# A four-layer decoder on one core: GpSimd's convolution taps placed behind each group's variance root in the first attention block

## The chip, the cores and the metric

The kernel runs on one core of a Trainium2 chip. The metric is the device time of the whole program in microseconds (us), as the median of runs. The engines are called as in the profile: PE (TensorE) multiplies matrices, DVE (VectorE) and ACT (ScalarE) work element by element and can read the results of PE, POOL (GpSimd) works on memory only, and SP (SyncE) issues transfers. Each engine runs its own instructions in order, and waits on semaphores for the others. All transfers of this stage are issued by SP.

## The reference

A decoder of four layers over 16 sequences of 128 tokens with 128 channels. Every layer has three blocks (attention, cross attention, feed-forward), and every block ends in `x = layernorm(x + block(x))`. The first attention block is

```
qkv = x @ W_qkv                                  # 16 heads of 8 channels
attn = softmax(mask(q @ k.T * SCALE))            # inside chunks of 64 tokens, causal
out_local = attn @ v
cross = sigmoid(q . mean_k(previous chunks) * SCALE)
out = (out_local + cross * cum_mean_v * 0.5) @ W_out
x = layernorm(x + out)                           # (x - mean) / sqrt(var + 1e-5)
```

The last layer's cross attention holds a long convolution (a diagonal state-space filter) whose 128 taps a channel depend on weights alone:

```
dtA = exp(log_dt) * (A_re + i A_im);  dC = C * (exp(dtA) - 1) / A
taps[d, l] = 2 * Re(sum_n dC[d, n] * exp(dtA[d, n] * l)),  n = 64 states, l = 0..127
```

with the skip weight added to the first tap.

## The kernel before, in words

`program` (L5379) runs the blocks one behind the other. Each is a `stage` (L35): five instruction streams between two common barriers. The change is in `small_heads` (L763), which makes the first attention (`local` is true) and the second layer's cross attention (`local` is false).

The 16 sequences go in four groups g = 0 to 3 of four sequences. A group has 16 units (head sets), and a written-out order of slots t sets what each engine does: at slot t PE makes the scores of one unit and the turned scores of a unit six slots older, DVE takes the maxima (`peak`, L1082), ACT the exponentials (`exp`, L1004), and one "misc" item of a group is made: input turned (`x`), projections (`q`, `k`, `v`), maxima and sums turned (`mt`, `ot`, L921), the output projection with the residual (`fin`, L981). The misc items share three PSUM banks in rotation, so an item waits until the item three before it has been moved out. DVE's `key_means` (L1090) makes the chunk means of the keys.

The layer norm of a group is spread over three engines:
- DVE's `moments(g)` takes statistics from the `fin` bank and aggregates them to mean and variance (`mv`, L1141), one slot behind `fin`.
- POOL computes the root of the variance: `rs = (var + eps) ** -0.5` and `nb = -mean * rs`, four small instructions (L1191 to L1197), here called root g. They wait for the variances of group g, and for g > 0 until the `fin` bank of group g − 1 was moved.
- ACT's `apply(g)` (L1051), three slots behind `fin`, writes `x_all` from the bank with that scale and bias. ACT's next exponential stands behind it, and the bank is free only then.

Besides, POOL computes in this stage the taps of the last layer's convolution, in class `Taps` (L610): `angles` and `powers` (L683 to L746) make tables of powers of the states, `low` (16 powers) and `high` (8). `taps(pool, a)` (L748) makes 16 of the 128 taps, for a = 0 to 7: one product over 128 x 2048 elements (L655), six halving sums (L658), one last sum to `kern`, and for a = 0 the skip. After a = 7 a small memset raises `made`, on which SP stores `kern` to DRAM (`store`, L635 to L638). Each instruction of the chain waits for the one before it.

POOL's order in this stage is: masks, `angles`, `powers`, taps 0 and 1, root 0, taps 2 and 3, root 1, taps 4 and 5, root 2, taps 6 and 7, root 3. SP's is: the parameters of the taps, the next block's weights, the store of the taps.

Of the kernel before, what the change touches and what calls it, by code (L numbers as in the profile page):

```python
# [762 lines left out]
def small_heads(K, pre, local):  # L763
# [10 lines left out]
    with ExitStack() as es:  # L774
# [64 lines left out]
        with stage(nc, *names) as (block, loaded, const_step, inited, pool_step, masks, filled, moved0, moved1, moved2, a_done, maxed, b_done, exped, o_done,  # L839
# [6 lines left out]
            s4d = Taps(K, sb, taps_loaded, dt_ready, angle, curves_made, tap_step, taps_made, taps_stored) if local else None  # L846

            @block.sync
            def _(sp):
                if local:  # L850
                    s4d.fetch(sp)
                    with nc.allow_non_contiguous_dma(reason="small parameter columns"):
                        K.w_l0_xattn.fetch(sp, I, next_in)
                    s4d.store(sp)
                    sp.wait_ge(next_in, 16 * K.w_l0_xattn.N)
                else:
                    for dst, n in ((wq_, "Wq"), (wk_, "Wk"), (wv_, "Wv"), (wo, "Wo")):
                        sp.dma_start(dst[:], I[pre + n]).then_inc(loaded, 16)
                    sp.dma_start(bo[:], row(I[pre + "bo"])).then_inc(loaded, 16)
# [303 lines left out]
            @block.gpsimd  # L1163
            def _(pool):
                if local:
                    build = Chain(pool, pool_step)
                    for full, low, turned in ((half_mask, mask16, False), (half_mask_t, mask_t16, True)):
                        sign = -1 if not turned else 1
                        build(nc.gpsimd.memset(full[:], 0.0))
                        for z in range(2):  # L1170
                            part = full[CS * z:CS * z + CS, :]
                            build(nc.gpsimd.affine_select(out=part, in_=part, compare_op=ALU.is_ge, fill=NEG, base=0,
                                                          pattern=[[sign, CS]], channel_multiplier=-sign))
                        build(nc.gpsimd.tensor_copy(low[:], full[:]))
                    build(nc.gpsimd.memset(to_next[:], 0.0))
                    nc.gpsimd.memset(to_next[0:CS, CS:T], 0.25 / CS).then_inc(masks, 1)
                    nc.gpsimd.memset(pT[:], 0.0).then_inc(masks, 1)
                    s4d.begin(pool)
                    s4d.angles(pool)
                    s4d.powers(pool)  # L1180
                for g in range(NG):
                    if local and g:
                        s4d.taps(pool, 2 * g)
                        s4d.taps(pool, 2 * g + 1)
                    if local and g == 0:
                        s4d.taps(pool, 0)
                        s4d.taps(pool, 1)
                    pool.wait_ge(var_ready, G * (g + 1))
                    if g:
                        wait_moved(pool, "fin", g - 1)  # L1190
                    nc.gpsimd.tensor_scalar(rs[:], mv[:, :, 1], EPS, None, ALU.add).then_inc(rstd_step, 1)  # L1191
                    pool.wait_ge(rstd_step, 3 * g + 1)
                    nc.gpsimd.tensor_tensor(rs[:], rs[:], K.minus_half[:, 0:G], ALU.pow).then_inc(rstd_step, 1)
                    pool.wait_ge(rstd_step, 3 * g + 2)
                    nc.gpsimd.tensor_scalar(nb[:], mv[:, :, 0], -1.0, 1.0, ALU.mult, ALU.mult).then_inc(rstd_step, 1)
                    pool.wait_ge(rstd_step, 3 * g + 3)
                    nc.gpsimd.tensor_tensor(nb[:], nb[:], rs[:], ALU.mult).then_inc(rstd_ready, 1)  # L1197
# [4248 lines left out]
```

## Time and profile before

| | us |
|---|---|
| median of 3 runs | 5502.06 (5499.12 to 5502.11) |
| profiled execution, its time | 5501.84 |
| its span, first to last instruction | 5500.1 |
| PE busy | 4484.7 (82%) |
| DVE busy | 3591.8 (65%) |
| ACT busy | 2738.8 (50%) |
| POOL busy | 2465.6 (45%) |
| mean granted clock of PE | 0.897 of full |

The busy times are of all twelve blocks together. The first attention block takes the stretch from 6 to 218 us of the span; ACT's first instruction of the next one starts at 220.25. A timeline row gives the start, the duration, the engine, the line, the operation, the tile written and the tiles read, the shapes, how many equal instructions were merged, and in brackets the idle time before it with what ended it. Where instructions of one line are merged, the duration is that of all of them. A row by stretches gives the stretch, its length, then the busy us and (in brackets) the instructions of PE, of PE's weight loads, of DVE, ACT and POOL, then the granted clock as a share of full (0.50 is 1.2 GHz, 1.00 is 2.4 GHz), and the share and GB/s of the DMA engines. In a list of waits, "A <- B" means that A's instruction waited for B's. In the code that follows a program's tile `s4prod` appears in rows as `l_attn_s4prod`.

### The profile page before, as it was taken

How to read it: one execution, taken by the hardware profiler on the slowest of the kernel's cores; microseconds unless marked ns; L12 is line 12 of the kernel's file. 1: busy time of each engine (PE TensorE's matmuls, PEld its weight loads, DVE VectorE, ACT ScalarE, POOL GpSimd, SP SyncE). 2: the span in 40 equal slices, each digit the busy share in tenths (PEclk: the TensorE clock that was granted, in tenths of full speed). 3: DMA queues.
4: the chain of work that ended last, by engine and by line, in shares of the span. 5: the costliest groups of instructions: out<-in, count | busy, mean ns of one | idle time of the engine just before them, and what ended most of it. 6: DMA issues, size and time to landing. Idle time of an engine off the chain costs nothing. (4 is left out here: it accounts for less than half of the span.)

```text
span 5500.1 us, 116174 instructions
## 1 busy us (share of the span) xinstructions
PE 4484.7 (82%) x45623; PEld 2775.8 (50%) x45624; DVE 3591.8 (65%) x6873; ACT 2738.8 (50%) x4638; POOL 2465.6 (45%) x2282
## 2 busy tenths in 40 slices
PE   7768999999999999678647888877887689967577
PEld 5545666666666666336523334343563444424344
DVE  4347777777777776475286999999553436547355
ACT  3325666666666666553225656655553235533121
POOL 8436666666666665250275666666332210001100
PEclk7789999999999999788668999999998779977788
DMA  1001111111111111000000000000000000020000
GB/s 23 16 29 28 45 37 29 49 33 45 36 43 37 29 37 29 5 0 3 12 1 14 0 1 1 0 1 1 15 1 0 13 9 16 1 70 5 20 1 8
DMA packets 110396, 102.35 MB, mean 19 GB/s; under 512 B 37095, under 2 KB 80375, under 8 KB 109111
## 3 DMA queue, kind: packets, MB, share of 16 engines
q1 hardware_dynamic: 107831, 94.14, 6.9%
q8 instruction: 357, 5.85, 0.4%
q0 software_dynamic: 2048, 1.05, 0.1%
q14 instruction: 160, 1.31, 0.1%
HBM read 40.18 MB, written 1.18 MB: 8 GB/s over the span
## 5 line engine op out<-in xcount | busy, mean ns | idle before, releaser
L4201 POOL TENSOR_TENSOR l_attn_read<-l_attn_state,l_attn_c_rows 128x1024 f32<-128x1024 f32 x256 | 604.4, 2362 | 291.6 <-DVE l_attn_state L4103 174.4
L2999 POOL TENSOR_TENSOR l_ffn_t<-l_ffn_t 128x512 f32<-128x512 f32 x384 | 487.3, 1269 | 506.5 <-DVE l_ffn_t L2866 506.5
L2597 PE MATMUL psum<-l_ffn_wq,l_ffn_xsT 128*128 128x512 f32 x1152 | 599.6, 612 | 99.3 <-DVE l_ffn_t L2866 97.8
L3823 PE MATMUL psum<-l_attn_read,ident 128*128 128x512 f32 x1024 | 489.9, 596 | 7.3 <-DVE l_attn_yz L4111 5.0
L3005 POOL TENSOR_TENSOR l_ffn_t<-l_ffn_t,l_ffn_ss 128x512 f32<-128x512 f32 x384 | 400.5, 1043 | 0.7 <-DVE l_ffn_ss L2881 0.7
L2862 DVE TENSOR_TENSOR l_ffn_t<-psum,l_ffn_tab 128x512 f32<-128x512 f32 x384 | 258.8, 674 | 121.3 <-ACT l_ffn_sq L2748 118.6
L4103 DVE TENSOR_TENSOR_SCAN l_attn_state<-l_attn_decay,psum 128x1024 f32<-128x1024 f32 x144 | 329.0, 2285 | 4.5
L2645 PEld LDWEIGHTS psum<-l_ffn_pT,l_ffn_v 64*64 64x64 f32 x3072 | 248.8, 135 | 142.9 <-issue 138.8
L2597 PEld LDWEIGHTS psum<-l_ffn_wq,l_ffn_xsT 128*128 128x128 f32 x1152 | 179.4, 191 | 274.0 <-DVE l_ffn_t L2866 237.9
L3979 ACT ACTIVATE l_attn_decay<-l_attn_dt,l_attn_a 128x1016 f32<-128x1016 f32 x256 | 292.9, 1144 | 37.2 <-DVE l_attn_state L4100 33.8
L2645 PE MATMUL psum<-l_ffn_pT,l_ffn_v 64*64 64x64 f32 (+1 forms) x3072 | 306.1, 227 | 1.2 <-ACT l_ffn_pT L2764 1.2
L2645 PE MATMUL psum<-l_ffn_pT,l_ffn_vx 64*64 64x32 f32 (+1 forms) x6144 | 303.6, 217 | 0.0
L4004 ACT COPY l_attn_c_rows<-psum 128x512 f32<-128x512 f32 x256 | 149.4, 584 | 298.9 <-PE psum L3814 263.1
L2220 ACT ACTIVATE l_attn_pT<-psum 128x512 f32<-128x512 f32 x320 | 173.6, 594 | 240.8 <-PE psum L2118 170.8
L2645 PEld LDWEIGHTS psum<-l_ffn_pT,l_ffn_vx 64*64 64x64 f32 x6144 | 282.3, 135 | 0.0
L4100 DVE TENSOR_TENSOR_SCAN l_attn_state<-l_attn_decay,psum 128x512 f32<-128x512 f32 x224 | 261.6, 1208 | 31.2 <-PE psum L3853 26.8
L3814 PE MATMUL psum<-l_attn_parts,pick 96*128 96x512 bf16 x456 | 170.6, 390 | 136.3 <-DVE psum L4086 88.7
L2748 ACT ACTIVATE l_ffn_sq<-psum 128x512 f32<-128x512 f32 x384 | 229.6, 598 | 103.7 <-PE psum L2597 103.6
L3823 PEld LDWEIGHTS psum<-l_attn_read,ident 128*128 128x128 f32 x1024 | 195.5, 192 | 140.0 <-issue 116.8
L2771 ACT COPY l_ffn_oT<-psum 128x512 f32<-128x512 f32 x192 | 111.9, 583 | 305.9 <-PE psum L2645 305.8
L4086 DVE TENSOR_TENSOR psum<-psum,l_attn_du 128x1024 f32<-128x1024 f32 x200 | 246.6, 1233 | 26.5 <-POOL l_attn_du L4178 4.6
L2866 DVE TENSOR_TENSOR l_ffn_t<-psum,l_ffn_tab 128x512 f32<-128x512 f32 x384 | 261.4, 681 | 0.0
(908 smaller groups left out, 11415.5 us busy)
## 6 DMA issues: line engine op xcount, KB each, us to landing
l_ffn_vx<-l_ffn_v SPq DMA_DIRECT2D x192, 128.0 KB
l_ffn_vx<-l_ffn_v SPq DMA_DIRECT2D x384, 64.0 KB
l_ffn_wq<-in_L_ffn_Wqkv SPq DMA_DIRECT2D x6, 1536.0 KB, 6.3
l_xattn_toep<-s4d_taps SPq DMA_DIRECT2D x4, 2048.0 KB, 17.1
l_ffn_wo<-in_L_ffn_Wo SPq DMA_DIRECT2D x6, 512.0 KB, 4.1
l_ffn_w<-in_L_ffn_W SPq DMA_DIRECT2D x6, 341.0 KB
l_ffn_w<-in_L_ffn_w SPq DMA_DIRECT2D x3, 512.0 KB, 4.1
x_all<-in_x SPq DMA_DIRECT2D x4, 256.0 KB, 4.2
```

What stands on the lines that cost most here:

```text
L2597: nc.tensor.matmul(ring[it % 2], xsT[:, n % 2, m % G, :], w, start=True, stop=True).then_inc(itemed, 1)
L2645: last = nc.tensor.matmul(OT[r, i * T + at:i * T + at + n], kinds[par][r, 4 * c + i, :], pT[r, i, at:at + n], start=True, stop=True)
L2862: nc.vector.tensor_tensor(t1[:, m % G, i, :].rearrange("p (h d) -> p h d", d=dh), dots.rearrange("p (h d) -> p h d", d=dh), rows(tab[:, z, ...
L2866: nc.vector.tensor_tensor(t2[:, x % 3, :].rearrange("p (h s d) -> p h s d", s=2, d=32), swapped_halves(dots, 8), tab[:, z, 2 * k + 1, :].r ...
L2999: nc.gpsimd.tensor_tensor(t1[:, m % G, i, :], t1[:, m % G, i, :], t2[:, x % 3, :], ALU.add).then_inc(added, 1)
L3005: nc.gpsimd.tensor_tensor(t1[:, m % G, i, :].rearrange("p (h d) -> p h d", d=dh), t1[:, m % G, i, :].rearrange("p (h d) -> p h d", d=dh), ...
L3823: last = nc.tensor.matmul(total[:, h * GT:(h + 1) * GT], K.ident[:], read[:, k % 3, h * GT:(h + 1) * GT], start=(n == 0), stop=(n == N - 1 ...
L3979: nc.scalar.activation(decay[:, k % 3, :, :, 1:T], dt[:, g % 2, :].rearrange("p (h g t) -> p h g t", h=2, g=G)[:, :, :, 1:T], ACT.Exp, sca ...
L4086: nc.vector.tensor_tensor(drive.rearrange("p (h n) -> p h n", h=2), rows(b_bank, 2), du[:, g % 2, :].rearrange("p (h n) -> p h n", h=2), A ...
L4100: nc.vector.tensor_tensor_scan(state[:, k % 3, at], decay[:, k % 3, h, :, :].rearrange("p g t -> p (g t)"), drive[:, at], 0.0, ALU.mult, A ...
L4103: nc.vector.tensor_tensor_scan(state[:, k % 3, :], decay[:, k % 3, :, :, :].rearrange("p h g t -> p (h g t)"), drive, 0.0, ALU.mult, ALU.a ...
L4201: nc.gpsimd.tensor_tensor(read[:, k % 3, :].rearrange("p (h n) -> p h n", h=2), state[:, k % 3, :].rearrange("p (h n) -> p h n", h=2), row ...
```

## The change

In POOL's stream of the first attention block the eight taps are dealt out anew. Before the wait for group g's variances there stand, for g = 1 to 3, the taps 3(g − 1) to 3g − 1, as far as there are eight; for g = 0 none. POOL's order becomes: masks, `angles`, `powers`, root 0, taps 0 to 2, root 1, taps 3 to 5, root 2, taps 6 and 7, root 3. The instructions themselves, their number and all other engines' streams stay the same, and so does the second user of `small_heads`, which has no taps.

```diff
                 for g in range(NG):
                     if local and g:
-                        s4d.taps(pool, 2 * g)
-                        s4d.taps(pool, 2 * g + 1)
-                    if local and g == 0:
-                        s4d.taps(pool, 0)
-                        s4d.taps(pool, 1)
+                        for a in range(3 * (g - 1), min(3 * g, s4d.HI)):
+                            s4d.taps(pool, a)
                     pool.wait_ge(var_ready, G * (g + 1))
                     if g:
                         wait_moved(pool, "fin", g - 1)
```

## Rows read from the trace of the kernel before

**Rows 1.** Waits, 0 to 219 us: who waited for whom: total us, times, longest.
```profile
ACT x_all L1051 <- POOL l_attn_nb L1197: 27.2, 2, 19.5
...
POOL l_attn_rs L1191 <- DVE l_attn_mv L1141: 5.8, 1, 5.8
```

**Rows 2.** Busy time by stretches (columns as told under the table above).
```profile
21.00:48.00 27.00, 26.91 (x317) 18.90 (x317) 10.49 (x20) 8.10 (x19) 21.28 (x34) 0.50 0.01 2
...
94.20:113.70 19.50, 0.00 (x0) 0.00 (x0) 0.00 (x0) 0.01 (x1) 17.90 (x22) 0.57 0.00 0
...
115.70:120.50 4.80, 4.80 (x62) 3.93 (x64) 1.55 (x4) 0.76 (x2) 4.72 (x2) 0.50 0.00 0
...
121.00:154.50 33.50, 29.76 (x698) 22.22 (x690) 17.09 (x44) 19.41 (x46) 18.77 (x19) 1.00 0.01 3
...
155.00:161.50 6.50, 6.50 (x104) 4.98 (x106) 1.63 (x4) 0.76 (x2) 5.95 (x8) 0.50 0.01 3
```

**Rows 3.** Timeline of POOL, 88 to 129 us: start, us, instruction.
```profile
88.61 1.49 POOL L746 TENSOR_SCALAR l_attn_s4high<-l_attn_s4high 128x512 f32<-128x512 f32 x1
...
90.18 4.51 POOL L655 TENSOR_TENSOR l_attn_s4prod<-l_attn_s4low,l_attn_s4high 128x2048 f32<-128x2048 f32 x1
...
101.11 4.49 POOL L655 TENSOR_TENSOR l_attn_s4prod<-l_attn_s4low,l_attn_s4high 128x2048 f32<-128x2048 f32 x1
...
111.76 0.23 POOL L1191 TENSOR_SCALAR l_attn_rs<-l_attn_mv 128x4 f32<-128x4 f32 x1
...
113.64 4.51 POOL L655 TENSOR_TENSOR l_attn_s4prod<-l_attn_s4low,l_attn_s4high 128x2048 f32<-128x2048 f32 x1
...
124.36 4.53 POOL L655 TENSOR_TENSOR l_attn_s4prod<-l_attn_s4low,l_attn_s4high 128x2048 f32<-128x2048 f32 x1
```

**Rows 4.** Timeline of ACT: L1004 exponentials, L1051 the apply.
```profile
60.79 0.77 ACT L1004 ACTIVATE l_attn_pT<-psum 64x256 f32<-64x256 f32 x2 [0.67 <-PE psum L902]
...
63.83 0.77 ACT L1004 ACTIVATE l_attn_pT<-psum 64x256 f32<-64x256 f32 x2 [2.28 <-PE psum L902]
...
93.44 0.77 ACT L1004 ACTIVATE l_attn_pT<-psum 64x256 f32<-64x256 f32 x2 [0.66 <-PE psum L902]
...
113.72 1.50 ACT L1051 ACTIVATE x_all<-psum,l_attn_nb,l_attn_rs 128x128 f32<-128x128 f32 x4 [19.51 <-POOL l_attn_nb L1197]
...
124.25 0.77 ACT L1004 ACTIVATE l_attn_pT<-psum 64x256 f32<-64x256 f32 x2 [0.55 <-PE psum L902]
...
152.71 1.50 ACT L1051 ACTIVATE x_all<-psum,l_attn_nb,l_attn_rs 128x128 f32<-128x128 f32 x4
...
156.51 0.77 ACT L1004 ACTIVATE l_attn_pT<-psum 64x256 f32<-64x256 f32 x2 [2.29 <-PE psum L902]
...
161.92 0.77 ACT L1004 ACTIVATE l_attn_pT<-psum 64x256 f32<-64x256 f32 x2 [4.65 <-PE psum L902]
...
163.84 0.77 ACT L1004 ACTIVATE l_attn_pT<-psum 64x256 f32<-64x256 f32 x2 [0.54 <-PE psum L902]
...
188.86 1.50 ACT L1051 ACTIVATE x_all<-psum,l_attn_nb,l_attn_rs 128x128 f32<-128x128 f32 x4
...
216.51 1.50 ACT L1051 ACTIVATE x_all<-psum,l_attn_nb,l_attn_rs 128x128 f32<-128x128 f32 x4 [7.68 <-POOL l_attn_nb L1197]
```

**Rows 5.** Timeline of DVE: L1141 variances, L1090 the key means.
```profile
82.30 1.59 DVE L1090 TENSOR_SCALAR l_attn_kmean<-head,l_attn_ksum 128x16 f32<-128x16 f32 x4
...
89.49 0.38 DVE L1141 BATCH_NORM_AGGREGATE l_attn_mv<-l_attn_st 128x2 f32<-128x6 f32 x4
...
140.79 0.65 DVE L1090 TENSOR_SCALAR l_attn_kmean<-head,l_attn_ksum 128x16 f32<-128x16 f32 x4
...
147.97 0.38 DVE L1141 BATCH_NORM_AGGREGATE l_attn_mv<-l_attn_st 128x2 f32<-128x6 f32 x4
```

**Rows 6.** Waits of SP's queue, 0 to 300 us.
```profile
SPq L637 <- POOL l_attn_s4t L760: 191.1, 1, 191.1
...
SPq L39 <- DMA s4d_taps<-l_attn_s4kern: 1.3, 1, 1.3
```

## The prediction, made before the changed kernel was timed

> **What bounds the kernel now.** The change touches one of the program's twelve blocks, the first attention, so the page's totals over 5500 us say little; the views to read are those of the stretch 0 to 219 us, in this order. First the list of waits: its longest single wait of ACT is 19.5 us, for POOL's last instruction of the variance root (the `nb` product) [rows 1]. Next the table by stretches: from 94.2 to 113.7 us PE, DVE and ACT do nothing at all and POOL works 17.9 of 19.5 us [rows 2]. So in this stretch POOL alone bounds the block. POOL's own timeline says with what: its last powers instruction starts at 88.61 and lasts 1.49, then come taps 0 and 1 (90.18 and 101.11), and only at 111.76 the root of group 0 [rows 3]. ACT's timeline shows the other end: the exponential before the apply starts at 93.44 and lasts 0.77, so ACT is ready at 94.21 and applies at 113.72, 19.51 us later [rows 4]. DVE's shows that the root's input was there: the four variances of group 0 are aggregated from 89.49 for 0.38, to 89.87 [rows 5]. The stall happens once: in groups 1 and 2 ACT goes from exponential to apply without waiting (the apply of group 1 starts at 152.71), since POOL has finished its taps by then.
>
> **The change part by part.**
> *Taps 0 and 1 leave the place ahead of root 0.* They cost 111.76 − 90.18 = 21.58 us of POOL time there [rows 3]. Root 0 then starts at 90.18, because its variances are 0.3 us older [rows 5]. From its first instruction to the apply that it releases are 113.72 − 111.76 = 1.96 us, so it is done at 92.1. ACT comes at 94.21: the root is 2.1 us early and the whole wait of 19.51 us goes. What is late next is ACT itself, at its place in order, and PE behind it, as in groups 1 and 2. Nothing was done under the stall by any of the three engines [rows 2], so no work has to be made up for.
>
> *A clock term.* The stall also reordered PE's clock. The granted clock fell in the stall and PE came back at half (1.2 GHz) from 115.7 to 120.5; in group 1, without a stall, it also fell, and ran at half from 155 to 161.5, full (2.4 GHz) between [rows 2]. After the change group 0 should look like group 1. From apply to the third exponential behind it the stalled group took 124.25 − 113.72 = 10.53 and the unstalled one 163.84 − 152.71 = 11.13 [rows 4]: 0.60 us are given back. Bounds: if the clock does not fall, the gap between the exponentials at 156.51 and 161.92, 5.41 us at half, becomes 3.04 as between 60.79 and 63.83, where the same slot ran at full [rows 4]: 2.4 us less, for each of the two groups. If it falls for twice as long, about 3 us more. I take 0.60, since group 1 is the nearest case.
>
> *Three taps go between roots 0 and 1, three between 1 and 2, two between 2 and 3* (before: two each). A tap takes 101.11 − 90.18 = 10.93 (the first, with the skip term), 10.65 for the second, and 124.36 − 113.64 = 10.72 beside work of the other engines [rows 3]. POOL is free from 92.06 (root 0 occupies it 113.64 − 111.76 = 1.88) and has three taps done by 92.06 + 32.3 = 124.4. The variances of group 1 were there at 147.97 + 0.38 = 148.35 [rows 5]; 18.9 us earlier is 129.45. Root 1 is on time with 5.1 us to spare, done at 131.4, and ACT wants it at 152.71 − 18.9 = 133.8. Next three taps: 131.4 + 32.2 = 163.6. Group 2's variances were there at 184.87 + 0.38 = 185.25 [rows 5], after the change at 166.35: POOL has 2.8 us to spare. The root is done at 168.3, and ACT wants it at 188.86 − 18.9 = 170.0 [rows 4]. Behind root 2 two taps remain, as before, and POOL waited 5.8 us ahead of root 3 [rows 1], which it keeps. So the added tap in each interval is hidden by POOL's own idle time. Without that cover (5.1 and 2.8 us, plus some 2 us each until ACT comes), every us by which taps are longer goes on the path.
>
> *The side of the taps' result.* SP waits 191.1 us for the last tap to store it [rows 6]. That tap keeps its place between roots 2 and 3; POOL waited 5.8 us behind it [rows 1] and the root took 1.96 more, so the store is issued some 8 us ahead of the last apply (216.51, for 1.50) [rows 4], and this moves with the rest. No DMA is issued from the code that moves; POOL's queue carries no transfer here, and SP's next transfers belong to the next stage, whose start moves as a whole. Cost nothing; only a last tap more than those 8 us later would let the store hold the stage.
>
> *DVE beside a busier POOL.* The 21.6 us of taps that ran alone now run beside attention. DVE's four small `kmean` instructions take 1.59 us in all beside POOL's work and 0.65 with POOL idle [rows 5]; the ones of the last group now meet a tap: +0.94. But from those lines to the variances that follow it is 89.49 − 82.30 = 7.19 us in the one case and 147.97 − 140.79 = 7.18 in the other, so the 0.94 was hidden. I take 0, bounds 0 and 1 us a group.
> The Trainium skill (GPSIMD Engine Reference, section 8, Key points) says that GpSimd shares its SBUF interfaces with VectorE and contends with VectorE instructions in a 2-port mode or with two SBUF inputs. For DVE the `kmean` pair agrees. That it would slow the taps is not seen: 4.49 us for the product with all engines still, 4.51 and 4.53 beside them. It speaks against the change all the same and is the second rival.
>
> **Sum.** 19.51 − 0.60 = 18.9 us. The profiled execution took 5501.84 us (span 5500.1), 0.2 below the median 5502.06: 5501.84 − 18.9 = 5482.9, or 5483.1 on the median. I say 5483.0, 0.34% faster. Stages run behind one another with a common end, so what this one saves arrives at the end.
>
> **The rivals.**
> 1. *Part of the gain is given back.* Everything later begins 18.9 us earlier, and the clock's falls may meet other work there. Against it: the three runs before spread over only 3.0 us. For it: two falls in this stage are worth 2.4 us each, and there are many later. Loss of 3 to 14 us: 5486 to 5497, typically 5490.
> 2. *The taps slow down beside attention, and the stall moves to roots 1 to 3: slower.* With a tap of τ us, root 1 is late by 3τ − 39.8 (92.06 + 3τ + 1.93 against 133.8), root 2 by 3τ − 34.3 and root 3 by 2τ − 27.2. That is nothing up to 11.4, 10.7 us at 14 (5494) and passes 18.9 at τ = 15.0, from where the change is slower; at 16 it costs 26.7 and gives 5510. The rows say 10.72 at most.
> 3. *The clock falls and stays down: slower.* Half clock stretched a slot by 5.41/3.04 = 1.78. If group 0's fall lasts until the next apply, the 33.5 us from 121 to 154.5 [rows 2] pay 0.78 each, 26.1 us, of which 2.4 are in the forecast: 5507. It is slower than before when 21.3 us are paid, behind 27 us of such work (49 us of half clock). For it: from 21 to 48 us PE ran at half for the whole stretch, busy 26.9 of 27 us [rows 2]. Against it: after both falls in full pipeline it rose again within 7 us of work.
> 4. *The change does not free the root*, because something else held it: 5502. Against it: variances at 89.87, and POOL's unbroken row of taps [rows 3, 5].
>
> **How the numbers follow.** A measurement of this kernel tells about 0.2% (11 us) from no change, so faster means below 5491. Forecast 0.81 (its own range 5478 to 5487); rival 1 0.10; rival 2 0.03, a half of it slower; rival 3 0.03; rival 4 0.03. Faster: 0.81 and over half of rival 1, 0.88. Slower: rival 3 and half of rival 2, about 0.04. The rest 0.08. The range reaches down to both falls gone and some luck, 5477, and up to rival 1's middle, 5490.
>
> **What would show it.** Right: ACT's apply of group 0 at 94.2 with no wait, root 0 at 90.2, the stage ending near 199 instead of 218, roots 1 and 2 behind an idle POOL. The clock term: half clock for about 6 us near 97. Wrong: POOL going from a tap straight into root 1 or 2 with ACT waiting; taps above 11.4 us; a half clock from 97 past 110; or a stage 19 us shorter in a program that is not.

## The result, and the profile after

The changed kernel takes 5479.69 us (median of 11 runs, 5470.66 to 5495.5), the kernel before 5502.06 (11 runs, 5493.73 to 5508.3). The ratio is 0.9961, 95% interval 0.9953 to 0.9969: 21.5 us faster, with 17 to 26 us in the interval. A second series gave 5479.88 us and 0.9960 (0.9946 to 0.9974). Forecast were 5483.0 and 18.9 us.

One more row of the kernel before, on which the prediction rests: the variances of group 2 in DVE's timeline of the kernel before.

```profile
184.87 0.38 DVE L1141 BATCH_NORM_AGGREGATE l_attn_mv<-l_attn_st 128x2 f32<-128x6 f32 x4
```

Of the kernel after, first the waits of the first 200 us. What answers to the 19.5 us of [rows 1] is gone. One wait of ACT for POOL's last root instruction is left, that of root 3 at the end of the block; before it was 7.7 us long [rows 4].

```profile
ACT x_all L1051 <- POOL l_attn_nb L1194: 5.9, 1, 5.9
```

POOL's timeline (start, us, instruction, idle time before it) answers to [rows 3]: behind the last powers instruction comes root 0 at once, or rather when its variances are there, for now POOL waits for DVE and not the reverse. Then tap 0, and roots 1, 2 and 3, each behind idle time.

```profile
88.58 1.49 POOL L746 TENSOR_SCALAR l_attn_s4high<-l_attn_s4high 128x512 f32<-128x512 f32 x1
...
92.99 0.23 POOL L1188 TENSOR_SCALAR l_attn_rs<-l_attn_mv 128x4 f32<-128x4 f32 x1 [2.93 <-DVE l_attn_mv L1141]
...
94.87 4.51 POOL L655 TENSOR_TENSOR l_attn_s4prod<-l_attn_s4low,l_attn_s4high 128x2048 f32<-128x2048 f32 x1
...
131.13 0.23 POOL L1188 TENSOR_SCALAR l_attn_rs<-l_attn_mv 128x4 f32<-128x4 f32 x1 [3.83 <-issue]
...
166.56 0.23 POOL L1188 TENSOR_SCALAR l_attn_rs<-l_attn_mv 128x4 f32<-128x4 f32 x1 [1.44 <-issue]
...
191.30 0.23 POOL L1188 TENSOR_SCALAR l_attn_rs<-l_attn_mv 128x4 f32<-128x4 f32 x1 [1.38 <-DVE l_attn_mv L1141]
```

ACT's timeline answers to [rows 4]. The first apply follows the exponential of 96.41 without idle time, 16.5 us earlier than before, the second 17.4, the third 18.8, the last 23.3 us earlier.

```profile
96.41 0.77 ACT L1004 ACTIVATE l_attn_pT<-psum 64x256 f32<-64x256 f32 x2 [0.66 <-PE psum L902]
...
97.21 1.50 ACT L1051 ACTIVATE x_all<-psum,l_attn_nb,l_attn_rs 128x128 f32<-128x128 f32 x4
...
106.89 0.77 ACT L1004 ACTIVATE l_attn_pT<-psum 64x256 f32<-64x256 f32 x2 [0.55 <-PE psum L902]
...
135.35 1.50 ACT L1051 ACTIVATE x_all<-psum,l_attn_nb,l_attn_rs 128x128 f32<-128x128 f32 x4
...
170.03 1.50 ACT L1051 ACTIVATE x_all<-psum,l_attn_nb,l_attn_rs 128x128 f32<-128x128 f32 x4
...
193.25 1.50 ACT L1051 ACTIVATE x_all<-psum,l_attn_nb,l_attn_rs 128x128 f32<-128x128 f32 x4 [5.92 <-POOL l_attn_nb L1194]
```

DVE's timeline answers to [rows 5]: the variances of group 0, and the last group's key means, which now meet a tap and take 1.68 us.

```profile
92.46 0.38 DVE L1141 BATCH_NORM_AGGREGATE l_attn_mv<-l_attn_st 128x2 f32<-128x6 f32 x4
...
123.43 1.68 DVE L1090 TENSOR_SCALAR l_attn_kmean<-head,l_attn_ksum 128x16 f32<-128x16 f32 x4
```

The table by stretches answers to [rows 2] (columns as there). In the stretch in which only POOL worked all engines work. Between 50 and 192 us the granted clock is at half (1.2 GHz) in four short stretches, one of them (77 to 83) ahead of anything that was changed, and it comes back to full (2.4 GHz) in the last part already at 182.5; before it did so at 212.5. The fall at 77 to 83 us is no effect of the change: the third profile of the kernel before has one at 78 to 81 us.

```profile
77.00:83.00 6.00, 6.00 (x92) 3.49 (x96) 0.65 (x2) 3.73 (x7) 5.04 (x13) 0.50 0.01 3
...
97.20:113.70 16.50, 14.94 (x322) 11.38 (x326) 6.12 (x14) 7.79 (x19) 15.64 (x12) 0.90 0.01 2
...
101.00:103.50 2.50, 2.50 (x36) 2.15 (x36) 0.69 (x1) 0.12 (x1) 2.34 (x3) 0.50 0.02 7
...
138.50:141.50 3.00, 3.00 (x35) 2.65 (x32) 1.12 (x2) 0.76 (x2) 2.84 (x3) 0.51 0.00 0
...
173.00:182.50 9.50, 9.38 (x129) 6.89 (x125) 0.55 (x2) 3.65 (x10) 8.93 (x8) 0.51 0.01 2
```

### The profile page after: what moved, and what is told of

Same layout as the page of the kernel before. It is cut to its first block and busy times, and to the rows that moved or that the text cites. A ratio compares the mean times of both kernels' runs of the same rounds, so it can differ in the third digit from the quotient of the medians.

```text
span 5479.9 us, 116175 instructions
## 1 busy us (share of the span) xinstructions
PE 4479.7 (82%) x45624; PEld 2775.0 (51%) x45624; DVE 3589.8 (66%) x6873; ACT 2739.1 (50%) x4638; POOL 2465.7 (45%) x2282
## 3 DMA queue, kind: packets, MB, share of 16 engines
q0 software_dynamic: 2048, 1.05, 0.1%
## 5 line engine op out<-in xcount | busy, mean ns | idle before, releaser
L2594 PE MATMUL psum<-l_ffn_wq,l_ffn_xsT 128*128 128x512 f32 x1152 | 603.1, 615 | 97.2 <-DVE l_ffn_t L2863 95.8
L3976 ACT ACTIVATE l_attn_decay<-l_attn_dt,l_attn_a 128x1016 f32<-128x1016 f32 x256 | 292.9, 1145 | 36.2 <-DVE l_attn_state L4097 32.8
```

What stands on the lines that cost most here:

```text
L2594: nc.tensor.matmul(ring[it % 2], xsT[:, n % 2, m % G, :], w, start=True, stop=True).then_inc(itemed, 1)
L3976: nc.scalar.activation(decay[:, k % 3, :, :, 1:T], dt[:, g % 2, :].rearrange("p (h g t) -> p h g t", h=2, g=G)[:, :, :, 1:T], ACT.Exp, sca ...
```

## The experiments

All ratios are against the kernel before, run on the same chip. A difference from the changed kernel's 5479.69 us compares the medians of two series; for one tap ahead, no taps, five taps, the product twice and the last two taps behind they are 9.4, 0.0, 18.2, 27.6 and 27.3 us, and by the ratios they would be 9, 5, 19, 24 and 24 us. So up to 5 us of them are not firm. "Block" is the start of ACT's first instruction of the next block (220.25 before), "rest" is the span less that.

**One tap ahead of root 0.**
```diff
-                    if local and g:
-                        for a in range(3 * (g - 1), min(3 * g, s4d.HI)):
+                    if local:
+                        for a in ([0], [1, 2], [3, 4, 5], [6, 7])[g]:
```


> Tap 0 stands ahead of root 0, tap 1 behind it (taps per place: 1, 2, 3, 2). Theory A (the gain is the stall of ACT's first apply, and that stall is what stands ahead of root 0 on POOL): root 0 starts where tap 1 started before, at 101.1, and is done at 103.1, ACT is ready at 94.2 to 97.2, so it waits 6 to 9 us, and the kernel is 10 to 13 us faster than before, near 5491, and 9 to 12 us slower than the changed one. Theory B (what counts is how taps are dealt out between the later roots, or that POOL is done earlier at the end): within 3 us of the changed kernel.

5489.1 us (10 runs), ratio 0.9977 (0.9967 to 0.9986): 12.7 us faster than before, 9.4 slower than the changed kernel. The root starts at 101.39, behind the tap, and ACT waits 5.62 us (POOL's and ACT's timelines). That is a little under the 6 to 9 us expected, because ACT was ready at 97.74 and not between 94.2 and 97.2.

```profile
101.39 0.23 POOL L1188 TENSOR_SCALAR l_attn_rs<-l_attn_mv 128x4 f32<-128x4 f32 x1
```
```profile
103.36 1.51 ACT L1051 ACTIVATE x_all<-psum,l_attn_nb,l_attn_rs 128x128 f32<-128x128 f32 x4 [5.62 <-POOL l_attn_nb L1194]
```

The gain follows what stands ahead of root 0. Theory B is out.

**No taps.**
```diff
-                    if local and g:
-                        for a in range(3 * (g - 1), min(3 * g, s4d.HI)):
-                            s4d.taps(pool, a)
+                    if local and g == 3:
+                        s4d.step(nc.gpsimd.memset(s4d.kern[:, 0:T], 0.0))
+                        nc.gpsimd.memset(s4d.t2[:, 0:1], 0.0).then_inc(s4d.made, 1)
```


> Leaves out the computation of all eight taps (the convolution's kernel is zeros, stored as before), the rest is the changed kernel. Theory A: the taps are wholly hidden behind the other engines once root 0 is free, so the time is that of the changed kernel within 1.5 us, and the first block is as long but for the clock's falls. Theory C (taps beside attention slow DVE or delay roots): over 3 us faster than the changed kernel, and the four key-mean instructions of DVE take 0.65 us in place of 1.68.

5479.71 us (5 runs), ratio 0.997 (0.9952 to 0.9987), against 5479.69 of the changed kernel: no difference that these runs can tell, though the interval is 19 us wide and does not by itself shut out the 3 us of theory C. The profile says more. The last group's key means take 0.65 us here, as theory C has it, but the block gains nothing by it: from apply to apply it takes 41.2, 36.2 and 26.7 us without taps, against 38.1, 34.7 and 23.2 in the first profile of the changed kernel and 41.1, 36.1 to 36.2 and 27.6 in the second and third. So the eight taps, some 86 us of POOL (8 x 10.7), cost nothing that can be measured, and a loss of over 3 us, as theory C has it, is not seen.

**Five taps between roots 0 and 1.**
```diff
-                    if local and g:
-                        for a in range(3 * (g - 1), min(3 * g, s4d.HI)):
+                    if local:
+                        for a in ([], [0, 1, 2, 3, 4], [5, 6, 7], [])[g]:
```


> Five taps between roots 0 and 1, three between 1 and 2 (taps per place: 0, 5, 3, 0). By the sum of the prediction root 1 is done at 92.1 + 10.9 + 4 x 10.7 + 1.9 = 147.8, ACT wants it at 133.8: 14 us of wait there, none at root 2 (three taps fit), so about 14 us slower than the changed kernel, 5494 to 5497. If POOL's place in the order only matters for root 0 (theory B2), no slower than the changed kernel.

5497.85 us (10 runs), ratio 0.9995 (0.9985 to 1.0004). It is 18.2 us slower than the changed kernel, where about 14 were expected, and a little above the range given. POOL goes from a tap straight into root 1, and ACT waits 15.40 us there.

```profile
148.90 0.23 POOL L1188 TENSOR_SCALAR l_attn_rs<-l_attn_mv 128x4 f32<-128x4 f32 x1
```
```profile
150.85 1.50 ACT L1051 ACTIVATE x_all<-psum,l_attn_nb,l_attn_rs 128x128 f32<-128x128 f32 x4 [15.40 <-POOL l_attn_nb L1194]
```

Root 1 was done at 150.8, 3.0 us later than summed, because root 0 had begun 2.9 us later (93.12 for 90.18, behind its variances); ACT was ready at 135.45 for 133.8, so the wait is 15.4 for 14. The stall can be moved from root 0 to root 1, and most of the gain goes with it; theory B2 is out.

**The product of every tap twice.**
```diff
         self.mul(prod[:], self.low[:].rearrange("p b c n -> p b (c n)"), rows(self.high[:, a, :, :].rearrange("p c n -> p (c n)"), LO))
+        self.mul(prod[:], self.low[:].rearrange("p b c n -> p b (c n)"), rows(self.high[:, a, :, :].rearrange("p c n -> p (c n)"), LO))
```


> The changed kernel with each tap's product of 2048 columns computed twice (same result), so that a tap takes 15.2 us in place of 10.7. By the lateness sum of the second rival root 1 is late by 3 x 15.2 - 39.8 = 5.8, root 2 by 3 x 15.2 - 34.3 = 11.3, root 3 by 2 x 15.2 - 27.2 = 3.2: 20.3 us in all, so within 3 us of the kernel before (5500 to 5505). If the idle time of POOL is larger than the sum says: under 15 us slower than the changed kernel.

5507.31 us (10 runs), ratio 1.0004 (0.999 to 1.0018): 27.6 us slower than the changed kernel, where 20.3 were summed. Root 2 made ACT wait 9.35 us (11.3 summed) and root 3 12.65 (its usual 7.7 and 5.0; 3.2 summed). But root 1 did not make ACT wait, though 5.8 us were summed: POOL sat idle for 2.48 us ahead of it, because DVE came later still. The timeline of DVE (the second row is the first of the four instructions alone) and of POOL:

```profile
123.41 9.12 DVE L1091 TENSOR_SCALAR l_attn_kmean<-head,l_attn_ksum 128x16 f32<-128x16 f32 x4
...
123.41 4.40 DVE L1091 TENSOR_SCALAR l_attn_kmean<-head,l_attn_ksum 128x16 f32<-128x16 f32 x1
```
```profile
123.26 9.10 POOL L655 TENSOR_TENSOR l_attn_s4prod<-l_attn_s4low,l_attn_s4high 128x2048 f32<-128x2048 f32 x2
...
140.94 0.23 POOL L1189 TENSOR_SCALAR l_attn_rs<-l_attn_mv 128x4 f32<-128x4 f32 x1 [2.48 <-issue]
```

Four instructions of 16 columns took 9.12 us, about as long as the two products that POOL executed beside them (123.26 to 132.36). From the first apply to the second it was 51.6 us (93.79 to 145.40) against 38.1, 41.1 and 41.1 in the three profiles of the changed kernel, so 10 to 14 us more. Of this the key means are 8.5 (9.12 against 0.65 with POOL idle); the rest is not taken apart, and PE's granted clock was at half (1.2 GHz) from 133 to 139 us. So in this interval the meeting of DVE's small instructions with POOL's long ones cost more than the lateness of 5.8 us that was summed for root 1; the lateness of roots 2 and 3 (9.35 and 5.0) makes up the rest of the loss.

**The product of tap 2 four times, whole, and in quarters.**
Whole: `for _ in range(4 if a == 2 else 1):` ahead of the product. In quarters, behind it:
```diff
+        if a == 2:
+            for part in (0, 1, 2, 3) * 3:
+                b = slice(4 * part, 4 * part + 4)
+                self.mul(prod[:, b], self.low[:, b].rearrange("p b c n -> p b (c n)"), rows(self.high[:, a, :, :].rearrange("p c n -> p (c n)"), 4))
```


> The changed kernel with the product of tap 2 alone computed four times (same result), so that POOL executes products of 2048 columns (4.5 us each) from about 117 to 135 us, when DVE's key means of the last group come (near 124). Theory D (such an instruction of DVE waits for the end of the POOL instruction that is executing): the four key-mean instructions take from 4.5 to 9.1 us together, the longest up to 4.5, and each long one ends with a product. Theory E (they are slowed in proportion while POOL is busy, as 1.68 against 0.65 us): under 2 us. Root 1 is later by 13.7 us of POOL work in both.

> As the one with tap 2's product four times, but the last three in quarters of 512 columns (1.3 us each), from about 121 to 137 us. Theory D: the key means meet short instructions and take at most two of them, 1.3 to 3 us together, the longest 1.3. Theory E: as in the whole-product kernel within a few tenths.

In the rows on the line of the key means (minimum, median and maximum in ns, over 118 to 140 us) the longest instruction takes 4529 ns beside whole products and 1296 beside quarters; the four together take 9.07 and 1.80 us.

```profile
L1091 DVE TENSOR_SCALAR l_attn_kmean<-head,l_attn_ksum x4: 221/2286/4529, 123.5 to 132.3; 128x16 f32<-128x16 f32 x4
```
```profile
L1094 DVE TENSOR_SCALAR l_attn_kmean<-head,l_attn_ksum x4: 221/270/1296, 128.1 to 129.7; 128x16 f32<-128x16 f32 x4
```

Beside whole products the first one starts at 123.49 and ends at 127.84, as the product of 123.29 does (127.80) and just before the next starts.

```profile
123.49 4.35 DVE L1091 TENSOR_SCALAR l_attn_kmean<-head,l_attn_ksum 128x16 f32<-128x16 f32 x1
```
```profile
123.29 4.51 POOL L655 TENSOR_TENSOR l_attn_s4prod<-l_attn_s4low,l_attn_s4high 128x2048 f32<-128x2048 f32 x1
...
127.88 4.51 POOL L655 TENSOR_TENSOR l_attn_s4prod<-l_attn_s4low,l_attn_s4high 128x2048 f32<-128x2048 f32 x1
```

Theory D holds: the instruction waits for the end of what POOL is executing. Two of the four were held, one for each product, and the other two took 0.22 us each, where a product had just ended. Theory E gave under 2 us for whole products.

One run of each took 5491.36 us (whole) and 5483.21 (quarters), beside 5496.37 of the kernel before. These 8 us are not a gain by the quarters: the block is 211.94 us with whole products and 213.89 with quarters, and only the unchanged rest of the program was shorter (5277.7 and 5267.6). With whole products root 1 did not make ACT wait, since DVE was late too; with quarters ACT waited 7.10 us for root 1, behind the added work on POOL.

**Every product twice, in quarters.** As the kernel with each product twice, but `for part in (0, 1, 2, 3) * 2` in place of the two products.

> As the kernel with the product computed twice, but each product in four instructions of 512 columns (1.3 us each in place of one of 4.5 us). Theory D (a key-mean instruction of DVE that comes while POOL executes an instruction with two inputs waits for that instruction's end): where these four instructions meet the products they take 4 x 1.3 = 5 us or less, in place of 9.1. Theory E (they are slowed in proportion while POOL is busy): 9 us as before. Taps take some 0.5 us each longer per product pair, 16 to 17 us, so roots 2 and 3 are later by 2 to 4 us more.

5517.12 us (one run). Inconclusive on D and E: the key means came at 125.12 beside the halving sums (121.97 to 127.73), not beside a product, and took 1.52 us. Taps of 17 us made roots 1, 2 and 3 late (ACT waited 9.39, 15.87 and 16.09 us, against 0, 9.35 and 12.65 with whole products twice); for roots 2 and 3 only 2 to 4 us more were expected.

**The last two taps behind root 3.**
```diff
-                    if local and g:
-                        for a in range(3 * (g - 1), min(3 * g, s4d.HI)):
+                    if local:
+                        for a in ([], [0, 1], [2, 3], [4, 5])[g]:
...
+                if local:
+                    s4d.taps(pool, 6)
+                    s4d.taps(pool, 7)
```


> Two taps behind each root, so the last two stand behind root 3 (taps per place: 0, 2, 2, 2, and 2 at the end). Root 0 is free as in the changed kernel, no other root is late, but the taps end 21.4 us behind root 3, and their store (some 2 us) holds the end of the block: 20 to 23 us slower than the changed kernel, so 0 to 4 us slower than before (5500 to 5506). If the next block's engines could start ahead of the store, the time is that of the changed kernel.

5507.04 us (10 runs), ratio 1.0005 (0.9993 to 1.0017): 27 us slower than the changed kernel, above the 20 to 23 expected. POOL ends the taps at 224.3, SP issues the store, and ACT, done with the block at 204.5, starts the next one at 228.46 (POOL's, SP's and ACT's timelines).

```profile
224.24 0.10 POOL L760 MEMSET l_attn_s4t<- 128x1 f32 x1
```
```profile
224.36 0.33 SPq L637 DMA_DIRECT2D s4d_taps<-l_attn_s4kern  x1
```
```profile
228.46 0.20 ACT L1425 ACTIVATE l_xattn_gamma<-l_xattn_gamma 128x1 f32<-128x1 f32 x1 [23.95 <-PEq L42]
```

So two taps in every place lose the whole gain to the block's end; the added tap in the first two places is what avoids it.

**Both kernels again.** No edit.

> The changed kernel a second time. Theory A with its clock part: ACT is ready for the first apply between 94 and 99 us, depending on where PE's clock fell in the 90 us before, and does not wait there; the first block takes 197 to 207 us, the rest of the program 5271 to 5283 us. The gain over the kernel before is 0.3 to 0.5% again. If the first profile's short last part (23.2 us from the third apply to the fourth, against 27.7 before) belongs to the change, it is short here too; if it was chance of the clock, it is 26 to 28 us.

> The kernel before a second time. The root of group 0 starts at 111.8 as it did, since POOL's work ahead of it depends on nothing else, and ACT waits for it from 94 to 99 us on: 14.7 to 19.5 us. The first block ends at 217 to 224 us. If the first pair's stall of 19.5 us was typical, it is over 18 again; if ACT's readiness moves with the clock's falls, it lies lower.

> The changed kernel a third time, for the spread of its parts. Expected from the two profiles before it: first block 197 to 207 us, the rest 5271 to 5284 us, ACT at the first apply between 94 and 99 us without a wait. If the gain were larger than the stall in truth, the block would be under 200 us again.

> The kernel before a third time. First block 217 to 222 us, a stall of 15 to 20 us at the first apply, the root of group 0 at 111.8; the rest 5271 to 5284 us.

Three profiles of each give, in us:

| | stall at the first apply | block | rest | span |
|---|---|---|---|---|
| before | 19.51, 20.06, 17.93 | 220.25, 221.63, 217.70 | 5279.9, 5284.2, 5277.8 | 5500.1, 5505.8, 5495.5 |
| after | none | 196.99, 205.05, 202.56 | 5282.9, 5274.1, 5280.0 | 5479.9, 5479.1, 5482.6 |

The stall and its absence, in ACT's timelines of the second profiles:

```profile
113.76 1.50 ACT L1051 ACTIVATE x_all<-psum,l_attn_nb,l_attn_rs 128x128 f32<-128x128 f32 x4 [20.06 <-POOL l_attn_nb L1197]
```
```profile
96.37 1.50 ACT L1051 ACTIVATE x_all<-psum,l_attn_nb,l_attn_rs 128x128 f32<-128x128 f32 x4
```

The stall is a property of the kernel before; its 20.06 us of the second profile lie just above the 14.7 to 19.5 expected. The last part of 23.2 us is not one of the kernel after: in the other two profiles it is 27.6 us (173.67 to 201.31 and 171.17 to 198.81), as before. The block is 219.9 us on average before and 201.5 after, 18.3 less. The rest, the same code in all, lies between 5267.6 and 5284.2 us over the fourteen profiles of this case: it moves by 16.6 us with nothing changed in it.

## Why the prediction was right

*The stall and what ends it.* This is the mechanism that was forecast, and it is shown. Root 0 stood behind 21.6 us of taps and ACT waited for nothing else. Shown from both sides: one tap left ahead of it leaves 5.62 us of stall, none leaves none, in all ten profiles without a tap ahead of it. The 19.51 us of the first profile were 17.9 to 20.1 in three.

*The added tap.* The margins were right in kind. In the three profiles after, POOL was idle ahead of root 1 for 3.8, 6.9 and 6.3 us (5.1 forecast) and ahead of root 2 for 1.4, 2.9 and 2.9 (2.8). Five taps in the first place bring the stall back at root 1; leaving all taps out brings nothing.

*The lateness sum of the second rival* had one wrong term. Roots 1 and 2 were counted from the time at which ACT wants the root before, root 3 from the time at which root 2 started in the kernel before (214.56 − 185.40 − 1.93 = 27.2). Once root 2 is late, ACT's own times count there too: 216.51 − 188.86 − 1.93 = 25.7, so root 3 is late by 2τ − 25.7. With taps of 15.2 us that gives 4.7; 5.0 were measured, and 3.2 summed.

*The store.* It moved with the rest, and holds the block only when taps stand behind root 3, as the sum said.

*The clock term* of 0.60 us is not confirmed. From the apply to the third exponential behind it three profiles before took 10.53, 11.49 and 11.00, three after 9.68, 11.09 and 12.55: means of 11.0 and 11.1, and a spread that hides the term. The half clock forecast for about 6 us near 97 came in all three profiles after, but for about 3, 7 and 10 us. What differs is where the clock's falls come. The first profile after had one at 77 to 83 us which the first before had not, in code that is the same: ACT reached the first apply at 97.21 and not at 94.21. Over all profiles ACT was ready between 93.7 and 99.1.

*DVE beside POOL* was the weak step. Its price of 0 held (1.68, 1.01 and 0.97 us for the key means in three profiles, and nothing gained without the taps), but the bound of "0 and 1 us a group", taken from the 1.59 us of [rows 5], was far too low: these four instructions can take 9.1 us. In the changed kernel they come at 123.43, 2.3 us behind the end of a product (116.59 + 4.53 = 121.12), and meet a halving sum instead. So the price of 0 was luck: it was right by place, not by principle. For the same reason the second rival was argued with the wrong victim: taps are not slowed (4.49 to 4.54 us a product throughout), DVE is held up.

*The sum.* 18.9 forecast, 21.5 measured with 17 to 26 in the interval, 18.3 in the block over three pairs. That the block comes within 1 us of the forecast is in part luck, since it moved by 8 us between the three profiles after. Whether the 3 us above the forecast are real stays open; the rest of the program varies by more from run to run.

## What to carry to other kernels

Where one engine serves a short, urgent step and long filler work, put the step ahead of the filler at the point where its input arrives, and then count how much filler fits into each interval; five taps ahead of one step cost most of the gain here, and two behind the last one all of it. One long wait in which PE, DVE and ACT all stand still was worth nearly its full length here (19.2 us on average, 18.3 gained in the block), and can be read from one row. When filler on GpSimd is moved, look also at which VectorE instructions it will lie beside: how long one of those is held goes by the length of a single GpSimd instruction, not by the total. Whether shorter GpSimd instructions make a whole block faster is not shown here.

## What was not expected of the hardware

A VectorE instruction of 16 columns, with its source in SBUF and taking 0.22 us alone, takes up to 4.53 us when GpSimd is executing a product of two SBUF inputs over 2048 columns, and 1.30 us at most when that product is cut to 512 columns: it ends when the GpSimd instruction ends. VectorE's instructions on PSUM in the same kernels are not touched (0.67 to 0.69 us for 512 columns either way), nor are the GpSimd products. Nor is every VectorE instruction that reads SBUF alone: the sum over the keys (256 columns of a tile in SBUF) lies beside quarter products and takes 0.42 us, as it does with GpSimd idle (0.42 at 140.3 us of the kernel before).

```profile
127.67 0.42 DVE L1092 TENSOR_REDUCE l_attn_ksum<-l_attn_k_dense 128x4 f32<-128x256 f32 x1 [0.67 <-ACT l_attn_k_dense L1040]
```

The Trainium skill (GPSIMD Engine Reference, section 8, Key points) states the contention, for VectorE instructions in a 2-port mode or with two SBUF inputs. These runs agree that only some VectorE instructions are held, and give the length of the hold, a wait to the end of the GpSimd instruction; in which mode the key means ran no trace here shows.

The rest of the program, 5268 to 5284 us of unchanged code, varies by about 0.3% between profiles, and in the first block the granted clock falls at other places from profile to profile. A difference of under 5 us between two single profiles of this kernel says nothing.
